# First layer's cross attention of a two-layer decoder: probabilities divided in token rows and packed by pairs of heads

## What is computed

```python
def xattn(x, ctx, bias, wq, wk, wv, wo):          # layer 0, cross attention
    q = einsum('bfd,dnh->bfnh', x, wq) * 16 ** -0.5
    k = einsum('btd,dnh->btnh', ctx, wk)
    v = einsum('btd,dnh->btnh', ctx, wv)
    weights = softmax(einsum('btnh,bfnh->bnft', k, q) + bias, axis=-1)
    attn = einsum('bnft,btnh->bfnh', weights, v)
    return einsum('bfnh,nhd->bfd', attn, wo)
```

## Time and profile before

| what | value |
|---|---|
| runs | 1675.7, 1675.9, 1676.32 us; median 1675.9 |
| span of the profiled execution (first to last instruction) | 1668.4 us, 7.5 below the median of the runs, which count what lies around the span |
| mean granted TensorE clock | 0.973 of full |
| PE, DVE, ACT, POOL busy | 1538.6, 979.4, 843.9, 466.9 us |
| layer 0 | from 0 to about 603 us |
| full groups (g = 3 to 7), from x_scores(0) to x_scores(0) | 60.5, 65.0, 65.0, 63.3, 54.4 us |
| group 8 (tail) | 39.2 us |

### The profile page before, as it was taken

How to read it: one execution, slowest core, us unless ns; L and a number is a source line. 1 busy time by engine, 2 the same in 40 slices (tenths; PEclk the granted TensorE clock), 3 DMA queues, 4 the chain that set the end, 5 groups by cost and what they waited for, 6 DMA issues and landing times. The chain is left out here.

```text
span 1668.4 us, 27286 instructions
## 1 busy us (share of the span) xinstructions
PE 1538.6 (92%) x10207; PEld 1083.6 (65%) x10207; DVE 979.4 (59%) x2295; ACT 843.9 (51%) x1849; POOL 466.9 (28%) x592
## 2 busy tenths in 40 slices
PE   8999999998987899999999999999999989996299
PEld 5777767766755677778777556665666654442288
...
GB/s 116 157 156 18 47 30 44 30 47 44 34 166 39 56 148 125 140 132 114 126 126 127 80 39 52 32 41 31 39 14 11 4 26 1 0 1 16 23 100 64
DMA packets 100929, 108.32 MB, mean 65 GB/s; under 512 B 25410, under 2 KB 89804, under 8 KB 100800
## 3 DMA queue, kind: packets, MB, share of 16 engines
...
## 5 line engine op out<-in xcount | busy, mean ns | idle before, releaser
L1789 POOL TENSOR_SCALAR c_pr<-c_pr,c_rsum 128x256 f32<-128x256 f32 x256 | 127.3, 512 | 185.0 <-DVE c_rsum L2205 184.7
L2083 ACT ACTIVATE c_pr<-bank,c_nmax 128x256 f32<-128x256 f32 x256 | 117.8, 472 | 118.4 <-DVE c_nmax L2200 118.3
L1520 ACT ACTIVATE b_G<-bank 128x320 f32<-128x320 f32 x128 | 55.9, 437 | 210.0 <-PE bank L1469 210.0
L1469 PE MATMUL bank<-b_XT,shared 128*128 128x320 f32 x512 | 154.2, 436 | 0.0
L2200 DVE TENSOR_REDUCE c_nmax<-bank 128x2 f32<-128x512 f32 x128 | 82.4, 685 | 104.1 <-PE bank L1848 104.0
L1483 PE MATMUL bank<-shared,b_G 128*128 128x256 f32 x640 | 142.2, 379 | 0.0
L1483 PEld LDWEIGHTS bank<-shared,b_G 128*128 128x128 f32 x640 | 121.2, 190 | 17.5
L1066 DVE TENSOR_TENSOR hT_all<-bank,a_causal 128x512 f32<-128x512 f32 x128 | 79.4, 682 | 68.4 <-PE bank L561 68.4
L496 POOL TENSOR_TENSOR a_L<-a_L,a_Lm 128x1232 f32<-128x1232 f32 x32 | 71.9, 2247 | 153.9 <-DVE a_Lm L1081 153.9
L1469 PEld LDWEIGHTS bank<-b_XT,shared 128*128 128x128 f32 x512 | 92.4, 192 | 27.3 <-issue 1.0
L1539 DVE COPY b_Y<-bank 128x256 f32<-128x256 f32 x80 | 33.9, 424 | 120.3 <-PE bank L1483 120.1
...
## 6 DMA issues: line engine op xcount, KB each, us to landing
...
```

The source lines that it names most:

```text
L1469: t = p.matmul(P[2 + n % 2][:, 0:HC], w1[e % 3][:, u, 128 * f:128 * f + 128], XT[e % 2][:, u, HC * m:HC * m + HC], start=(u == 0), stop=(u ...
L1789: p.tensor_scalar(pr[k][:, e, u, :], pr[k][:, e, u, :], rsum[k][:, e, u:u + 1], 1.0, ALU.mult, ALU.mult).then_inc(q.pr_ready, 1)
L2083: a.activation(pr[t % 2][:, e, u, :], P[e][:, S * u:S * u + S], ACT.Exp, bias=nmax[t % 2][:, e, u:u + 1], accum_out=sums[t % 2][:, e, u:u ...
```

## The change

It moves the division of the softmax before the turn, and so removes the way back to token rows:
- DVE sums the exponents of a tile in token rows (`sums`: a reduction and a reciprocal); POOL multiplies (`normalised`) into two new buffers, `Pm` (the first 64 keys) and `Pl` (the last 13).
- `x_turn` turns pairs of heads: 2 x 64 keys fill 128 rows, so eight transposes, and two for the tails of eight heads each (8 x 13 = 104 rows): 10 instead of 16, in three units instead of four.
- The values of a pair of heads lie block-diagonally: 128 rows (64 keys of each head) by 32 columns in `xvp`; the tail rows of eight heads by 128 columns in `xvl`, masked by `tailsel`. `x_values` makes two full products for the tails and adds eight column tiles, and its result is already what `project` needs (`axT`). One bank instead of two.
- xtok0 to 3, their divisions, xcol0 and xcol1 are gone.
- `x_rows_v` makes 2 + 4 products in place of 4; SP loads the first 64 context columns once more into `ctxm` (two more DMAs a group), ACT repeats the last 13 eight times into `ctxl` (`repeat_tail`), keeps `xvm` in four copies, DVE keeps `xvl` with a multiplication (`keep_x_tail`, two operations).

Places on the queues, after (before): PE: x_turn(0) at the end of step 4 (step 3), (1) end of 6 (5), (2) end of 0 (7), (3) end of 2 (1); x_values(0) end of 7 (6), x_values(1) at 3 (2); xproj0 at 1 (2), xproj1 at 5. DVE: sums(3) at step 1, (0) at 3 after moments(1), (1) at 5 before xproj1's addition, (2) at 7 before shifts(2) and weigh, each behind masked of the next tile; keep_x_tail at the end of 3. ACT: by_key(2) at 0, (3) at 2, (0) at 4, (1) at 6, each at the end; keep_x_values(0) first in 0, (1) in 3; repeat_tail at 1. Masked no longer waits for the turn two tiles before, but for its multiplication. The diff's core (the set-up of `tailsel` and the smaller fills on POOL left out):

```diff
+KM = 64
+KL = S2 - KM
...
-xvpad = [sb(f"xvpad_{k}", [S2, NB, H, 32]) for k in range(2)]
+xvp = [sb(f"xvp_{k}", [128, NB, H // 2, 2 * HD]) for k in range(2)]
+xvl = [sb(f"xvl_{k}", [8 * KL, NB, 2, 128]) for k in range(2)]
+tailsel = sb("tailsel", [128, 8])
+ctxm = sb("ctxm", [128, 2, NB, KM])
+ctxl = sb("ctxl", [128, 2, NB, 8, KL])
+Pm = sb("Pm", [128, H, KM])
+Pl = sb("Pl", [128, H, KL])
...
-PT = sb("PT", [S2, H, S])
+PTm = sb("PTm", [128, H // 2, S])
+PTl = sb("PTl", [8 * KL, 2, S])
...
+NTURN = 3
+
 def turned(j):
-    return tuple(f"xt{j}_{n}" for n in range(RG))
-
-UNITS = {0: (("xtok0", -3), ("xtok1", -3), ("k0", 1), ("k1", 1), ("tok2", -1), ("tok3", -1), ("xq1", -2)),
-         1: (("val0", 0),) + tuple((n, -3) for n in turned(3)) + (("col1", -1), ("xcol0", -3), ("xk", -1), ("v0", 1)),
-         2: (("proj1", -1), ("xproj0", -3), ("xval1a", -3), ("xval1b", -3), ("pkt", 1)),
-         3: (("val1", 0),) + tuple((n, -2) for n in turned(0)) + (("xtok2", -3), ("xtok3", -3), ("turn2a", -4), ("turn2b", -4), ("xv", -1)),
-         4: (("tok0", 0), ("tok1", 0), ("q0", 1), ("q1", 1), ("xcol1", -3), ("logits", -4)),
-         5: (("val2", 0),) + tuple((n, -2) for n in turned(1)) + (("col0", 0), ("xproj1", -3), ("v1", 1), ("gate", -4)),
-         6: (("proj0", 0), ("turn1a", -1), ("turn1b", -1), ("xval0a", -2), ("xval0b", -2), ("turn0a", 2), ("turn0b", 2),
-             ("rank", -4), ("state0", 1), ("state1", 1)),
-         7: (("val3", 0),) + tuple((n, -2) for n in turned(2)) + (("xq0", -1),)}
+    return tuple(f"xt{j}_{n}" for n in range(NTURN))
+
+UNITS = {0: (("k0", 1), ("k1", 1), ("tok2", -1), ("tok3", -1), ("xq1", -2)) + tuple((n, -3) for n in turned(2)),
+         1: (("val0", 0), ("col1", -1), ("xproj0", -3), ("xk", -1), ("v0", 1)),
+         2: (("proj1", -1), ("pkt", 1)) + tuple((n, -3) for n in turned(3)),
+         3: (("val1", 0), ("turn2a", -4), ("turn2b", -4), ("xval1", -3), ("xvm", -1), ("xvl", -1)),
+         4: (("tok0", 0), ("tok1", 0), ("q0", 1), ("q1", 1), ("logits", -4)) + tuple((n, -2) for n in turned(0)),
+         5: (("val2", 0), ("col0", 0), ("xproj1", -3), ("v1", 1), ("gate", -4)),
+         6: (("proj0", 0), ("turn1a", -1), ("turn1b", -1), ("turn0a", 2), ("turn0b", 2),
+             ("rank", -4), ("state0", 1), ("state1", 1)) + tuple((n, -2) for n in turned(1)),
+         7: (("val3", 0), ("xq0", -1), ("xval0", -2))}
...
+                s.dma_start(ctxm[:, u, :, :], ctx_cols[i, u, :, :, 0:KM]).then_inc(q.ctx_in, 16)
...
+        def normalised(i, j):
+            n = NT * i + j
+            p.wait_ge(q.xden_ready, n + 1)
+            if n:
+                wait_full(p, f"xt{(n - 1) % NT}_{NTURN - 1}", (n - 1) // NT)
+            p.tensor_tensor(Pm[:, :, :], L[n % 2][:, :, 0:KM], bcast(xrden[:, j, :], 2, KM), ALU.mult).then_inc(q.xn_ready, 1)
+            p.tensor_tensor(Pl[:, :, :], L[n % 2][:, :, KM:S2], bcast(xrden[:, j, :], 2, KL), ALU.mult).then_inc(q.xn_ready, 1)
...
             if s in (0, 1) and there(g - 5):
                 scatter(g - 5, s)
+            if s == 1 and there(g - 3):
+                normalised(g - 3, 3)
...
                 less_maximum(g - 2, 0)
...
+            if s == 3 and there(g - 2):
+                normalised(g - 2, 0)
...
+            if s == 5 and there(g - 2):
+                normalised(g - 2, 1)
...
+            if s == 7 and there(g - 2):
+                normalised(g - 2, 2)
...
         def x_rows_v(i):
-            room(p, "xv", i)
+
+            p.wait_ge(q.tail_ready, i + 1)
+            room(p, "xvm", i)
+            for u in range(2):
+                x = p.matmul(bank("xvm", i)[:, 0:D], ctxm[:, u, :, :].rearrange("p b k -> p (b k)"), xwv[:, u, :], start=(u == 0), stop=(u == 1))
+            x.then_inc(full("xvm", i), 1)
+            room(p, "xvl", i)
             for b in range(NB):
                 for u in range(2):
-                    x = p.matmul(bank("xv", i)[0:S2, D * b:D * b + D], ctxT[:, u, b, :], xwv[:, u, :], start=(u == 0), stop=(u == 1))
-            x.then_inc(full("xv", i), 1)
+                    x = p.matmul(bank("xvl", i)[0:8 * KL, D * b:D * b + D], ctxl[:, u, b, :, :].rearrange("p h k -> p (h k)"), xwv[:, u, :],
+                                 start=(u == 0), stop=(u == 1))
+            x.then_inc(full("xvl", i), 1)
 
         def x_turn(i, j):
+
             n = NT * i + j
-            p.wait_ge(q.exp_ready, n + 1)
-            for rg in range(RG):
-                name = f"xt{j}_{rg}"
+            p.wait_ge(q.xn_ready, 2 * n + 2)
+            for u in range(2):
+                name = f"xt{j}_{u}"
                 room(p, name, i)
-                for k in range(4):
-                    x = p.transpose(bank(name, i)[0:S2, 128 * k:128 * k + 128], L[n % 2][:, 4 * rg + k, :], ident)
+                for r in range(4):
+                    x = p.transpose(bank(name, i)[:, 128 * r:128 * r + 128], Pm[:, 8 * u + 2 * r:8 * u + 2 * r + 2, :].rearrange("p h k -> p (h k)"), ident)
                 x.then_inc(full(name, i), 1)
+            name = f"xt{j}_2"
+            room(p, name, i)
+            for u in range(2):
+                x = p.transpose(bank(name, i)[0:8 * KL, 128 * u:128 * u + 128], Pl[:, 8 * u:8 * u + 8, :].rearrange("p h k -> p (h k)"), ident)
+            x.then_inc(full(name, i), 1)
 
         def x_values(i, b):
+
+            name = f"xval{b}"
             for j in (2 * b, 2 * b + 1):
-                for rg in range(RG):
-                    wait_kept(p, f"xt{j}_{rg}", i)
-            wait_kept(p, "xv", i)
-            for half, tag in enumerate("ab"):
-                name = f"xval{b}{tag}"
-                room(p, name, i)
-                for k in range(2):
-                    for hh in range(4):
-                        h = 8 * half + 4 * k + hh
-                        x = p.matmul(bank(name, i)[32 * hh:32 * hh + 32, S * k:S * k + S], xvpad[i % 2][:, b, h, :], PT[:, position(h), :],
-                                     start=True, stop=True, tile_position=(0, 32 * hh))
-                x.then_inc(full(name, i), 1)
+                for n in range(NTURN):
+                    wait_kept(p, f"xt{j}_{n}", i)
+            wait_kept(p, "xvm", i)
+            wait_kept(p, "xvl", i)
+            room(p, name, i)
+            for u in range(2):
+                p.matmul(bank(name, i)[:, S * u:S * u + S], xvl[i % 2][:, b, u, :], PTl[:, u, :], start=(u == 0), stop=False,
+                         skip_group_check=True)
+            for u in range(2):
+                for r in range(4):
+                    x = p.matmul(bank(name, i)[32 * r:32 * r + 32, S * u:S * u + S], xvp[i % 2][:, b, 4 * u + r, :], PTm[:, 4 * u + r, :],
+                                 start=False, stop=True, tile_position=(0, 32 * r), skip_group_check=True)
+            x.then_inc(full(name, i), 1)
...
+        def repeat_tail(i):
+
+            a.wait_ge(q.ctx_in, 64 * (i + 1))
+            if i:
+                wait_full(a, "xvl", i - 1)
+            a.activation(ctxl[:, :, :, :, :].rearrange("p u b h k -> p (u b) h k"),
+                         bcast(ctxT[:, :, :, KM:S2].rearrange("p u b k -> p (u b) k"), 2, 8), ACT.Copy).then_inc(q.tail_ready, 1)
+
         def keep_x_v(i):
-            wait_full(a, "xv", i)
+            wait_full(a, "xvm", i)
             for b in range(NB):
-                x = a.activation(xvpad[i % 2][:, b, :, 0:HD], bank("xv", i)[0:S2, D * b:D * b + D].rearrange("p (h d) -> p h d", d=HD), ACT.Copy)
-            x.then_inc(freed("xv", i), 1)
+                for e in range(2):
+                    x = a.activation(xvp[i % 2][KM * e:KM * e + KM, b, :, HD * e:HD * e + HD],
+                                     bank("xvm", i)[KM * b:KM * b + KM, 0:D].rearrange("p (r e d) -> p r e d", e=2, d=HD)[:, :, e, :], ACT.Copy)
+            x.then_inc(freed("xvm", i), 1)
...
         def by_key(i, j):
-            for rg in range(RG):
-                name = f"xt{j}_{rg}"
-                keep(name, i, PT[:, 4 * rg:4 * rg + 4, 128 * (j % 2):128 * (j % 2) + 128], bank(name, i)[0:S2, :].rearrange("p (h t) -> p h t", h=4))
+            cols = slice(128 * (j % 2), 128 * (j % 2) + 128)
+            for u in range(2):
+                name = f"xt{j}_{u}"
+                keep(name, i, PTm[:, 4 * u:4 * u + 4, cols], bank(name, i)[:, :].rearrange("p (r t) -> p r t", r=4))
+            name = f"xt{j}_2"
+            keep(name, i, PTl[:, :, cols], bank(name, i)[0:8 * KL, 0:256].rearrange("p (u t) -> p u t", u=2))
...
             if n >= 2:
-                wait_full(v, f"xt{(n - 2) % NT}_{RG - 1}", (n - 2) // NT)
+                v.wait_ge(q.xn_ready, 2 * n - 2)
...
+        def sums(i, j):
+            n = NT * i + j
+            v.wait_ge(q.exp_ready, n + 1)
+            v.tensor_reduce(xrden[:, j, :], L[n % 2][:, :, :], AX.X, ALU.add).then_inc(q.xsum_ready, 1)
+            v.wait_ge(q.xsum_ready, n + 1)
+            v.reciprocal(xrden[:, j, :], xrden[:, j, :]).then_inc(q.xden_ready, 1)
+
+        def keep_x_tail(i):
+
```

(6 more changed lines are left out.)

125 lines of the change are left out of this document (52 added, 73 removed).

## The result

The changed kernel takes 1715.7 us (median of 4 runs) against 1675.8 for the kernel before: a ratio of 1.025, with a 95% interval of 1.0235 to 1.0265. It is **slower by 40 us**. The forecast was 1678 us with a range of 1662 to 1691, so the result lies outside it, and on the side of rival 2, beyond that rival's 1689.

What follows compares the result with a forecast made beforehand. A group's first part was taken as bound by PE, its second by DVE. Until group 7's last x_scores -17.6 us, tail +17.5, clock +2: sum +2 us, forecast 1678 us, range 1662 to 1691.

Steps and rivals of the forecast that it cites:

- rival 2: GpSimd's queue decides, in step 7 and behind the scatters: full hold +5, lower clock +6 more, 1689 us; chance 20%.
- The straight count of PE's work: PE's turns, removed transposes, value rows and values: -4.4 us a group, -35 us in eight.
- Full groups, first part: Steps 1 to 5 of a full group, bound by PE: -4.0 us.
- less 0.7 for waits on banks that DVE must free: First part of a full group: 0.7 us of the 4.7 saved goes to bank waits (tail multiplication, q features).
- Second part: Gate to the next group's first x_scores, bound by DVE: +1.8 us taken, between +0.5 and +2.9.
- the router's operations now meet two GpSimd operations in a row: Second part: tile 2's multiplications, then less_maximum of tile 3, may hold DVE by 0 to +2.4 us more.
- middle value of 1.8: Second part's change taken as +1.8 us, between +0.5 without further holding and +2.9 with all of it.
- the upper bound: Second part with DVE held in full by the added GpSimd operation: +2.9 us; the forecast would be 3 us later.
- The tail: Groups 8 to 10: one tile's chain exposed, last multiplication queued behind eight scatters; +17.5 us.
- The clock: Longer PE gaps in the tail lower its clock: +2 us taken, bounds 0 and +8.
- Rival 1: The gain outlives the tail, only half of its 17.5 us paid: about 1663 to 1667 us; chance 30%.
- Rival 3: Wide turns or 128-key tiles run slower than counted, +1 us per product set, +16: 1695 us; chance 3%.

Runs made afterwards that it cites:

- e17: Changed kernel, router first in full groups, idle transposes and last two groups' product on VectorE, bank passed over in step 2 (step 6 only without router): ratio 1.0057.
- e18: Changed kernel with the PSUM bank ring passing over the bank VectorE's residual addition still reads, in step 2, in step 6 only without router: ratio 1.0195.
- e16: Changed kernel without sums, reciprocals and product, turns reading undivided exponentials, plus the bank ring passing over the residual addition's bank in steps 2 and 6: ratio 0.9841.
- e14: Changed kernel with the ring of four PSUM banks passing over the bank VectorE's residual addition still reads, in steps 2 and 6: ratio 1.0172.
- The short product: Changed kernel with GpSimd's product cut to one key a head, still waited for by the turns, which read undivided exponentials: ratio 1.0044.

## Why the prediction was wrong

**The straight count of PE's work** was right. A turn of ten transposes takes 1.23 us up to the next operation (318.54 to 319.77) for 1.13 counted, the two full products and the eight column tiles of a product set take 0.96 and 1.00 us (306.40 to 308.36) for 0.97 and 1.0 counted, and a full group of e17 has PE busy for 58.3 us against 62.4, 4.1 less for 4.4 forecast.

**Full groups, first part**: forecast 35.8 us, measured 39.0 (287.25 to 326.21). The failed step is "less 0.7 for waits on banks that DVE must free". The bank ring was read for the units that come later, not for those that move closer to a slow reader; it cost one wait of 2.04 us in the group, with 4.2 us at a clock of 0.59 behind it, which is 1.7 us lost (an estimate: 0.41 of 4.2). Up to the last x_scores of group 7 the bank edit of e18 is worth 7.6 to 11.4 us on the changed kernel (457.7 instead of 469.1 and 465.3), and that of e16 9.4 on the undivided one (444.0 for 453.4, both marked). With both steps on the changed kernel (e14) only 1.0 to 4.8 us are seen there, in a marked set.

**Second part**: forecast 27.0 us (bounds 25.7 to 28.1), measured 32.35 (326.21 to 358.56). The failed step is the sentence that "the router's operations now meet two GpSimd operations in a row": true for the weights in step 7, but the product of tile 1 also pushes less_maximum of tile 2 from 318.84, before the choice, into the choice, one of whose operations it holds until its end (2.11 us for 0.17); this was overlooked, and leads to 3.04 us of wait at turn0b. And the middle value of 1.8 between "no further hold" and "all of it" was the wrong choice: in step 7 VectorE lost 1.7 + 0.3 + 2.0 us where it had lost 2.0: 2.0 more, nearly all of the 2.4 that was the forecast's bound.

The rule of the Trainium skill (page "SBUF — State Buffer", section "Who interferes with whom") that the later of the two blocks for the whole instruction fits all four rows, the conversion and the operation with one input included, which the page counts among those that can take the pair. By it the upper bound would have been the estimate, and still 4 us a group too low.

Up to the last x_scores of group 7 the forecast was -17.6 us and +18.2 came: 35.8 apart. The short product takes 21.2 of this away (447.9 for 469.1; 17.4 from the other profile), the bank some 9. If the two add, which no run shows, 5 to 9 us stay open.

**The tail** had the right mechanism and too small a size: +26.7 for +17.5 us. By pieces:

| piece | before | forecast | after |
|---|---|---|---|
| group 7 step 7 to group 8 step 3 | 25.9 | 27.2 | 25.8 |
| to group 8 step 7 | 19.4 | 21.0 | 26.6 |
| to group 9 step 7 | 38.6 | 46.1 | 50.1 |
| to the end of xproj1 | 31.0 | 38.1 | 39.2 |

The stretch around the scatters was sized well: from x_scores(3) to the next x_scores(1) it takes 26.7 us (521.45 to 548.17) for 26.9 forecast, and the last row is 1.1 us off. Missing is, again, the choice, whose mask the ranks need: PE waited for it 4.4 us in the second row and 5.7 in the third, 10.1 together, where these rows are 5.6 and 4.0 us over the forecast. Before the first of these waits the choice's two comparisons take 2.72 us instead of 0.36; the sums, which stand ahead of the choice, are the likely rest. VectorE and GpSimd there:

```profile
515.88 2.72 DVE L1200 TENSOR_TENSOR a_oh<-a_eid,a_topf 128x64 f32<-128x64 f32 x2
```

```profile
513.89 1.92 POOL L510 TENSOR_TENSOR a_Pm<-a_L,a_xrden 128x1024 f32<-128x1024 f32 x1 [5.27 <-DVE a_xrden L1118]
515.76 0.55 POOL L511 TENSOR_TENSOR a_Pl<-a_L,a_xrden 128x208 f32<-128x208 f32 x1
516.27 2.25 POOL L503 TENSOR_TENSOR a_L<-a_L,a_Lm 128x1232 f32<-128x1232 f32 x1
```

**The clock** was put in the tail, +2 us, and at nothing in the full groups. Raising it in the tail gained nothing that can be told. In the full group its three slow stretches (4.2, 4.7 and 4.7 us at 0.59, 0.64 and 0.64) cost PE about 5 us against full clock, an estimate from these rows; it fits that PE is busy for 63.3 us in these 72.0 and for 58.3 in e17's group at full clock. No run raised the clock in the full groups alone, so that this is lost time is not shown apart from the waits.

**Rival 2** named the mechanism but with a price of +5 us for the hold and +6 for the clock in the tail, when the product on GpSimd moved the middle alone by 14 us (206.8 against 192.8), with nobody waiting for it. **Rival 1** and the forecast shared the error of letting the gain of the full groups stand. **Rival 3** falls: wide transposes and 128-row tiles ran as counted.
